# A QR factorisation on GpSimd turned from columns on partitions to rows of 288, inside a four-layer transformer kernel

## The reference

```python
x = _L0_cond_ref(x, cond, ...)   # layer norm, attention (16 heads), top-2 of 4 experts
x = _L1_cond_ref(x, cond, ...)   # layer norm, attention, one MLP of 1152
x = _L2_cond_ref(x, cond, ...)   # the same
# _L3_cond_ref
U, _ = jnp.linalg.qr(P)
R = _rotation(cond, W, b)        # expm of a skew matrix, 64 x 64 per batch
z = jnp.einsum('btn,nd->btd', x, U)
z_rot = jnp.einsum('btd,bde->bte', z, R)
x_rot = x + jnp.einsum('btd,nd->btn', z_rot - z, U)
```

## Time and profile before

| | |
|---|---|
| median of 3 runs | 1878.96 us (1878.91 to 1879.99) |
| profiled execution, device time | 1883.78 us |
| its span, first to last instruction | 1882.1 us |
| outside the span | 1.7 us |
| mean granted TensorE clock | 0.961 |
| busy PE, DVE, ACT, POOL | 94%, 73%, 48%, 35% |

### The profile page before, as it was taken

One profiled execution on the slowest core, in us unless ns is written; L12 is line 12 of the kernel. 1 busy time (PEld: TensorE's weight loads), 2 busy tenths in 40 slices (PEclk: granted clock), 3 DMA queues, 4 the chain that ended last, 5 costly groups with the idle time before them and its releaser, 6 DMA issues.

```text
span 1882.1 us, 35890 instructions
## 1 busy us (share of the span) xinstructions
PE 1767.6 (94%) x11507; PEld 1167.8 (62%) x11507; DVE 1382.1 (73%) x2622; ACT 906.9 (48%) x1591; POOL 651.4 (35%) x1549
## 2 busy tenths in 40 slices
PE   6989999899999999999899999898989899989999
PEld 4753333698988888888673333487866233348885
DVE  7658886777888756567867888677886888867763
ACT  4617777433512311213555777633346477763322
POOL 1432333433444434433443233433443333334100
PEclk9969999899999999999988999899999899989999
DMA  6354220200120020100344221000014522100001
GB/s 167 97 146 140 76 74 21 67 1 14 64 66 1 2 67 1 36 1 1 106 146 127 67 76 57 27 10 1 14 45 139 154 66 75 57 1 1 1 1 51
DMA packets 61026, 106.44 MB, mean 57 GB/s; under 512 B 10997, under 2 KB 44595, under 8 KB 60779
## 3 DMA queue, kind: packets, MB, share of 16 engines
q1 hardware_dynamic: 60908, 104.87, 18.6%
HBM read 80.97 MB, written 23.67 MB: 56 GB/s over the span
## 4 chain that ended last, share of the span: by engine, by line
PE 73%; DVE 16%; ACT 4%; issue 3%; DMA 3%; SPq 1%; DVEq 0%; ACTq 0%
PE psum L856 23%; PE psum L1071 13%; PE psum L977 10%; PE psum L964 10%; PE psum L947 9%; PE psum L888 2%; DVE bn L1277 1%; PE psum L907 1%; PE psum L1096 1%; DVE hid_lo L1482 1%; PE psum L1009 1%; ACT x_mod L709 1%; DVE hid_hi L1481 1%; DVE branch L1503 1%; DMA qk_parts_d<-qk_parts 1%
## 5 line engine op out<-in xcount | busy, mean ns | idle before, releaser
L1349 DVE TENSOR_REDUCE row_max<-psum 128x2 f32<-128x1024 f32 x384 | 467.8, 1223 | 120.8 <-PE psum L947 120.5
L756 ACT ACTIVATE probs<-psum 128x512 f32<-128x512 f32 x768 | 445.3, 597 | 188.4 <-PE psum L964 180.0
L808 ACT ACTIVATE hid_f<-psum 128x512 f32<-128x512 f32 x216 | 128.8, 596 | 549.4 <-PE psum L856 536.1
L856 PE MATMUL psum<-x_split,w_hi 128*128 128x512 f32 x864 | 319.2, 410 | 3.6 <-DVE x_tail L1325 3.6
L964 PE MATMUL psum<-q_stack,k_stack 109*128 109x512 bf16 x768 | 291.8, 387 | 4.9 <-DMA q_stack<-row_max_t 2.7
L1071 PE MATMUL psum<-w_hi,hid_hi 128*128 128x288 f32 x864 | 259.2, 300 | 6.7 <-DVE hid_lo L1482 4.5
L947 PE MATMUL psum<-k_stack,q_stack 108*128 108x512 bf16 x768 | 248.3, 407 | 14.1 <-DVE qk_r L1339 6.7
L1071 PE MATMUL psum<-w_hi,hid_lo 128*128 128x288 f32 x864 | 256.5, 297 | 0.0
L1071 PE MATMUL psum<-w_lo,hid_hi 128*128 128x288 f32 x864 | 256.4, 297 | 0.0
L977 PE MATMUL psum<-probs,v_stage 128*32 128x256 f32 x3072 | 242.9, 391 | 1.1 <-ACT o_t L748 1.1
L1481 DVE CAST hid_hi<-hid_f 128x512 fp32r<-128x512 f32 x216 | 94.9, 439 | 162.5 <-ACT hid_f L808 135.0
(11 more groups left out here) (251 smaller groups left out, 2851.9 us busy)
## 6 DMA issues: line engine op xcount, KB each, us to landing
qk_parts_d<-qk_parts SPq DMA_DIRECT2D x72, 288.0 KB, 2.8
q_stack<-qk_parts_d SPq DMA_DIRECT2D x48, 216.0 KB
k_stack<-qk_parts_d SPq DMA_DIRECT2D x48, 216.0 KB
q_stack<-qk_parts_d SPq DMA_DIRECT2D x48, 144.0 KB
k_stack<-qk_parts_d SPq DMA_DIRECT2D x48, 144.0 KB
raw_b<-in_L_cond_w SPq DMA_DIRECT2D x5, 1296.0 KB
raw_a<-in_L_cond_w SPq DMA_DIRECT2D x5, 1152.0 KB
q_stack<-qk_parts_d SPq DMA_DIRECT2D x48, 72.0 KB
```

What stands on the lines that cost most here:

```text
L756: act.activation(PE_[:, v // 4, v % 4, :], psum[:, 4 + v % 2, :], ACT.Exp, scale=SCALE).then_inc(s_e, 1)
L808: act.activation(HF[:, i % 2, :], bk(i % 2), ACT.Gelu_apprx_tanh).then_inc(s_g, 1)
L856: i = pe.matmul(dst, a, r, start=(n == 0), stop=(n == len(terms) - 1))
L1349: dve.tensor_reduce(MX[:, g % 2, 2 * u:2 * u + 2], psum[:, o:o + 2, :], AX.X, ALU.max).then_inc(s_mx, 1)
```

## The change

The factorisation is laid out the other way: each of 64 partitions holds one column of P as a row of 288 numbers (tile `qr_rows`). The row of the pivot column is copied to all 64 partitions by a transfer that GpSimd issues, the dot products with it are a multiplication and a tree of additions along the row (halving the length), and the rows are updated in place. Nothing is summed over partitions. The loop is written out 64 times, with the active length 288 - k. The reflectors are not scaled in the loop but at the end (`scale_rows`). P has to be transposed for this: TensorE does it in `turn_p` between `turn(0, 0, 1)` and `qkv(0, 0)`, and VectorE copies the result out of PSUM behind `low(0, 0, 0)`. Ahead of its first value products TensorE waits for that copy (`s_pt`), since they overwrite the PSUM bank. The first two of the 18 steps of `u_step` change places, since now the rows exist and the columns have to be made from them by a transpose.

```diff
@@ gpsimd
-            reflectors(0, D3)
+            def reflector(k):
+                n, col = C - k, slice(k, k + 1)
+                rows, pivot = QX[:, 0, k:C], QX[:, 1, 0:n]
+                gp.dma_start(pivot, QX[k:k + 1, 0, k:C].unsqueeze(1).to_broadcast([1, D3, n])).then_inc(s_qb, 16)
+                gp.wait_ge(s_qb, 16 * (k + 1))
+                step(gp.tensor_tensor(QM1[:, 0, 0:n], rows, pivot, ALU.mult))
+                step(gp.tensor_tensor(QM1[:, 1, 0:n], pivot, pivot, ALU.mult))
+                settle()
+                while n > 1:
+                    h = n // 2
+                    step(gp.tensor_tensor(QM1[:, :, 0:h], QM1[:, :, 0:h], QM1[:, :, n - h:n], ALU.add))
+                    settle()
+                    n -= h
...
+                step(gp.tensor_tensor(nrm, s_, half, ALU.pow))
...
+                step(gp.tensor_tensor(rd, d_, mone, ALU.pow))
+                settle()
+                step(gp.tensor_scalar(w_, w0, rd, QMN[:, col], ALU.mult, ALU.mult))
+                settle()
+                step(gp.tensor_tensor(QM1[:, 0, 0:C - k], pivot, w_.to_broadcast([D3, C - k]), ALU.mult))
+                settle()
+                step(gp.tensor_tensor(rows, rows, QM1[:, 0, 0:C - k], ALU.add))
+                settle()
...
+            gp.wait_ge(s_pt, 1)
+            for k in range(D3):
+                reflector(k)
+            scale_rows()
@@ tensor
+                if l == 0 and b == 0:
+                    pe.wait_ge(s_pt, 1)
...
+            def turn_p():
+                pe.wait_ge(s_p, 16)
+                for c in range(3):
+                    i = pe.transpose(psum[0:D3, 5, 96 * c:96 * c + 96], PRAW[:, c, :], IDN[0:96, 0:96])
+                i.then_inc(s_pq, 1)
...
                     turn(l, 0, 1)
+                    turn_p()
                     qkv(l, 0)
@@ vector
                     split_lo_qkv(l, 0)
                     low(l, 0, 0)
+                    dve.wait_ge(s_pq, 1)
+                    dve.tensor_copy(QX[:, 0, :], psum[0:D3, 5, 0:C]).then_inc(s_pt, 1)
                     split_lo_qkv(l, 1)
```

More of the change, by code:

```diff
@@ L173, in build @@
         CW = new("expert_w", [P, NT, EXPERTS], F32)
-        QA = new("qr_a", [96, 3, D3], F32)
-        QV = new("qr_v", [96, 3, D3], F32)
-        QG = new("qr_rows_ge", [96, 3, D3], F32)
-        QO = new("qr_onehot", [96, D3], F32)
-        QM1 = new("qr_m", [96, 3, D3], F32)
-        QI = new("qr_in", [96, 2, D3], F32)
-        QS = new("qr_sums", [96, 2, D3], F32)
-        QC = new("qr_cols", [96, 24], F32)
-        QW = new("qr_w", [96, D3], F32)
+        QX = new("qr_rows", [D3, 2, C], F32)
+        PRAW = at("p_raw", [96, 3, D3], F32, top[0])
+        QM1 = new("qr_m", [D3, 2, C], F32)
+        QMN = new("qr_rows_gt", [D3, D3], F32)
+        QSN = new("qr_scale", [D3, 2, D3], F32)
+        QC = new("qr_cols", [D3, 12], F32)
         UO = new("skew_upper", [D3, B, D3], F32)
@@ L600, in _ @@
                              pattern=[[1, D3]], channel_multiplier=-1).then_inc(s_qr, 1)
+            gp.affine_select(out=QMN[:, :], in_=QMN[:, :], compare_op=ALU.is_gt, fill=0.0, base=0,
+                             pattern=[[-1, D3]], channel_multiplier=1).then_inc(s_qr, 1)
+            gp.memset(QC[:, 1:2], -0.5).then_inc(s_qr, 1)
+            gp.memset(QC[:, 2:3], -1.0).then_inc(s_qr, 1)
             gp.wait_ge(s_qr, 8)
-            half, vcol, oneh, sal = QC[:, 0:1], QC[:, 1:4], QC[:, 4:5], QC[:, 5:7]
@@ L650, in _, with step, settle @@
-            gp.wait_ge(s_p, 16)
-            reflectors(0, D3)
+            half, mhalf, mone, nrm, sg, t_, w0, w_, rd = (QC[:, i:i + 1] for i in range(9))
+            done = [8]
+            def step(i):
+                i.then_inc(s_qr, 1)
+                done[0] += 1
+            def settle():
+                gp.wait_ge(s_qr, done[0])
+            def reflector(k):
[11 more added lines that the diff above has]
+                    n -= h
+                dots, s_ = QM1[:, 0, 0:1], QM1[:, 1, 0:1]
+                al, sn, d_ = QX[:, 1, 0:1], QSN[:, 0, col], QSN[:, 1, col]
+                step(gp.tensor_tensor(nrm, s_, half, ALU.pow))
+                step(gp.tensor_scalar(sg, al, 0.0, 2.0, ALU.is_ge, ALU.mult))
+                settle()
+                step(gp.tensor_scalar(sn, sg, -1.0, nrm, ALU.add, ALU.mult))
+                settle()
+                step(gp.tensor_tensor(t_, al, sn, ALU.mult))
+                step(gp.tensor_tensor(w0, QX[:, 0, col], sn, ALU.mult))
+                settle()
+                step(gp.tensor_scalar(d_, t_, s_, TINY, ALU.add, ALU.max))
+                step(gp.tensor_tensor(al, al, sn, ALU.add))
+                step(gp.tensor_tensor(w0, w0, dots, ALU.add))
+                settle()
+                step(gp.tensor_tensor(rd, d_, mone, ALU.pow))
+                settle()
+                step(gp.tensor_scalar(w_, w0, rd, QMN[:, col], ALU.mult, ALU.mult))
+                settle()
+                step(gp.tensor_tensor(QM1[:, 0, 0:C - k], pivot, w_.to_broadcast([D3, C - k]), ALU.mult))
+                settle()
+                step(gp.tensor_tensor(rows, rows, QM1[:, 0, 0:C - k], ALU.add))
+                settle()
@@ new lines, in scale_rows @@
+            def scale_rows():
+                eye = IDN[0:D3, 0:D3].unsqueeze(1).to_broadcast([D3, 2, D3])
+                step(gp.affine_select(out=QX[:, 0, 0:D3], in_=QX[:, 0, 0:D3], compare_op=ALU.is_ge, fill=0.0, base=0,
+                                      pattern=[[1, D3]], channel_multiplier=-1))
+                step(gp.tensor_tensor(QSN[:, :, :], QSN[:, :, :], eye, ALU.mult))
+                settle()
+                step(gp.tensor_tensor(QX[:, 0, 0:D3], QX[:, 0, 0:D3], QSN[:, 0, :], ALU.add))
+                n = D3
+                while n > 1:
+                    n //= 2
+                    step(gp.tensor_tensor(QSN[:, 1, 0:n], QSN[:, 1, 0:n], QSN[:, 1, n:2 * n], ALU.add))
+                    settle()
+                step(gp.tensor_tensor(rd, QSN[:, 1, 0:1], mhalf, ALU.pow))
+                settle()
+                gp.tensor_tensor(QX[:, 0, :], QX[:, 0, :], rd.to_broadcast([D3, C]), ALU.mult).then_inc(s_u, 1)
@@ L1120, in u_step @@
                 elif n == 15:
-                    mm = pe.matmul(o, NW[:, 3, :], VTR[:, 0:D3], start=True, stop=True)
+                    mm = pe.matmul(o, NW[:, 3, :], QX[:, 0, 0:D3], start=True, stop=True)
                 elif n == 16:
-                    mm = pe.matmul(psum[0:D3, 3, 0:C], NW[:, 5, :], VTR[:, :], start=True, stop=True)
+                    mm = pe.matmul(psum[0:D3, 3, 0:C], NW[:, 5, :], QX[:, 0, :], start=True, stop=True)
                 else:
```

68 lines of the change are left out of this document (13 added, 55 removed).

## The result

The changed kernel took 1890.06 us in the median of six runs (1884.88 to 1894.54), the kernel before 1878.93 in the same series (1876.69 to 1879.99). The ratio is **1.0044, with a 95% interval of 1.0023 to 1.0065**: slower by 0.44%, about 8 us. The two medians alone stand 11.1 us apart (0.59%, inside the interval), so the size is known to a few us only. The forecast of 1882.5 was 1.0019; the range (1877 to 1888) goes up to 1.0048, so the ratio (1887.2) lies inside it and the median of the six runs 2 us above it; the chance given to "slower" was 0.4. The profiled execution took 1891.35 against 1883.8 for that of before, +7.6.

A forecast was written before the change was run, and what follows sets the result against it. The prediction took TensorE, busy 94% and 73% of the chain of waits, to bound the kernel. Start 3.0, clock 0.5 and contention 0 made +3.5 us, 1887.3 in the profiled execution's terms, 1882.5 against the median; range 1877 to 1888.

The forecast's parts named there:

- GpSimd's new pace: GpSimd's factorisation: 16 us a reflector (14.5 to 21.5), ending near 1055 us, so that `u_step` still doesn't wait.
- The late GpSimd: Rival, GpSimd's loop: code loads return, 29.5 us a reflector, `u_step` waits 108 us, time 1987 us; chance 0.03.
- The copy and its wait: Start of layer 0: VectorE waits for P's transposes and copies, delaying TensorE's fourth product by 3.0 us (2.4 to 3.6).
- The clock: Behind TensorE's longer pause at the start: part of the lower clock level repeats, +0.5 us (0 to 1.8).
- GpSimd beside VectorE: VectorE's operations beside GpSimd's: +1.6 us in layer 0, -1.6 after GpSimd ends, net 0 (-2 to +3).
- The third rival: Layer 0: VectorE's waits grow with GpSimd's operation length, +3.2 to +6 us, time 1885 to 1888; chance 0.27.
- The relief rival: After GpSimd ends, before layer 1's feed-forward: relief wins, sum +0.3 us, 1874 to 1876 with the stall given back; chance 0.1.

The follow-up runs named there:

- experiment 1: Reflectors left out, ratios to the kernel before: in the kernel before 1866.84 us, 0.9921; in the changed kernel, copy of P and its wait kept, 1871.74 us, 0.9957.
- experiment 2: Changed kernel with VectorE's copy of P moved behind the first query and key product's sums: 1888.93 us, 1.0041 of the kernel before.
- experiment 5: Changed kernel with GpSimd's wide operations in pieces of at most 72 columns, copy of P left in place: 1884.21 us, 1.0006 of the kernel before.
- the cut kernel: Changed kernel with VectorE's copy of P moved later and GpSimd's wide operations in pieces of at most 72 columns: 1873.67 us (0.997), again 1874.71 us (0.9955).
- the late copy: Changed kernel with VectorE's copy of P behind the first query and key product's sums: 1.0041 with whole operations, 0.997 and 0.9955 with pieces of 72 columns.
- the early one: VectorE's copy of P left where the change put it, with its wait: 1.0044 with whole operations, 1.0006 with pieces of at most 72 columns.

## Why the prediction went as it did

- **GpSimd's new pace: right, in part by luck.** 16 us a reflector and an end at 1055 were forecast, 16.1 and 1063.9 came; no stop of 6 us is left, and `u_step` does not wait. But two terms were off and nearly cancelled: the transfer, for which no row of before had a price, was taken as 3.5 us out of 2 to 9 and is 0.64 + 3.8, and the idle between steps, 2.9 in the sum, is 1.7 (the operations, 9.6 in the sum, are 9.9). The late GpSimd is out.
- **The copy and its wait: right, but not all of the delay.** The copy was to start at 30.4 and the product to come 3.0 us later; 30.68 and 4.8 us, of which the copy and its wait are 3.0. The forecast said that what is queued behind keeps its lengths; it does not, since GpSimd's first wide operations fall on VectorE's small ones (1.5 us). What the 4.8 us are worth in the kernel's time was not settled (experiments 1, 2 and 5); so that a delay at this place is on the path to the end, as the sum had it, is not shown.
- **The clock: +0.5 was not seen**, neither behind the longer pause (0.83 for 0.84) nor in the mean, 0.961 in both.
- **GpSimd beside VectorE: the term of the sum that was mis-sized.** "Net 0 (-2 to +3)" was made of +1.6 in layer 0 and -1.6 after it; in the profiled executions it is about +13 behind the start until 1044 us and -10 after 1064, +3 in all, the upper bound. With the start's 4.8 this makes the 7.6 of the profiled executions. But both halves were too small by a factor of six to eight. That the time still came out inside the range is luck: two large parts of opposite sign nearly cancelled, and the middle of 0 had no ground. The share of busy time, 0.60 / 0.40, was part of it: it came out at 0.69, and held time went from 21.1 to 43.8 us, a factor of 2.08 for one of 1.72 in the share. But a share is not what VectorE pays for. In the cut kernel the share is 0.75 and held time 16.4. Where I could assign held time to what GpSimd was doing at the moment (27.5 us of before, 49.6 of after; which operation holds a VectorE instruction is not in the trace, this is one way to share it out), that of before is the update `L647` (7.4), `L646` (3.8) and `L625` (4.2), all of 192 elements, and the sum over partitions (5.0); a line of 64 has 0.6 to 1.0, one of a single element at most 0.2. After, the tree has 16.5 and the four operations of up to 288 elements 8.7, 8.3, 7.2 and 6.7; all column operations and powers at most 0.2 each, though they last up to 0.7 us. Shared out by overlap instead, the tree has 19.4, the four 9.0 to 5.5 and a column operation or power at most 0.5: the same order.
- **Why both halves were small.** In layer 0 the base, 3.2 us, is near what the table has for before (+2.9), but its parts were not right. The 450 ns from which `branch` was counted belong to another form of it, the one of layers 1 and 2 without `expert_w`; without reflectors the layer 0 form takes 512, so that (559 - 512) x 64 = 3.0 us and not 7.0 were GpSimd's. `hid_lo` was given 0.3 us, and its share of the chain is 1.4% without reflectors, 2.1% before and 4.1% after, 8, 12 and 24 us. And the base was raised by half, with the share of busy time, where the loss went from +2.9 to +11.6. After layer 0 the forecast gave 1.0 us to layer 1's feed-forward part, where the table has 4.8 us of held time and 7.4 lost. In all it took GpSimd's work to cost the kernel before 4.8 us; experiment 1 has 15.
- **The third rival came true**, in its direction and, by the ratio, its time: 1885 to 1888, and 1878.93 x 1.0044 is 1887.2. Its sum was 3 to 6 us in layer 0 with nothing larger coming back, so the time is luck here too. Its mechanism, that what is lost grows with the length of the other's operation, is what the cut kernels show. The Trainium skill (SBUF — State Buffer, Who interferes with whom) has VectorE and GpSimd shut each other out for a whole instruction, if VectorE's reads two operands from SBUF or is a copy or cast in a fast mode, and never for a reduction; by it the term was to be at its upper end. The trace agrees: `hid_lo`, with two, +54 ns; `hid_hi`, a cast, +33 (442 and 475); `row_max`, a reduction out of PSUM, 1223 ns in both. Whether the cast runs in such a mode no row shows.
- **The relief rival** had its place right, the end of GpSimd's work ahead of layer 1's feed-forward part, and was beaten by layer 0 and the start.

Open: the price of the start's stall, from about nothing to 9 us, and so how the 8 us divide between the start and GpSimd's wider operations. By experiment 1 GpSimd costs both kernels nearly the same (15 and 16 us), by experiment 2 the start costs nothing; both can't be the whole. What is shown is that with the wide operations cut the slowdown is gone. Executions of one kernel also scatter by about ±0.5% within a series (1872 to 1890 us for the kernel before in later ones, against 1876.69 to 1879.99 here; 1864 to 1877 without reflectors), so that the profiled execution alone can stand several us from the median; verdicts here go by the ratios.

## What to carry to other kernels

An engine outside the chain of waits can still cost the kernel 15 us: price GpSimd's work by VectorE's rows beside it, and by the width of its single operations, not by its busy share; and take the undisturbed length of an instruction from the same form of it. When side work moves to wide elementwise operations, cut them into pieces of some 70 columns first; it costs GpSimd more instructions, and here turned +0.41% into -0.3 to -0.45% with the late copy, and +0.44% into +0.06% with the early one. Ask of each phase what a held microsecond costs there; whether side work is better ended before a phase that loses all of it is a question that these runs raise and do not settle.
